# Two diagonal cells joined into one, and other places for the second keys, the inverses and the Gelu, in a two-layer transformer kernel

## What is computed

```
x = x + 0.5 * fp4_ffn(norm(x))          # weights and activations rounded to a 4-bit grid, width 352
x = x + linear_attention(norm(x))       # 16 heads of 64, and a feed-forward of width 512
x = x + 0.5 * fp4_ffn(norm(x))
x = x + 0.5 * relu_ffn(norm(x))         # width 512
x = x + causal_attention(norm(x))       # below
x = x + 0.5 * relu_ffn(norm(x))
```

```
scores = Q K^T + mask (causal);  attn = softmax(scores);  o = attn V
out = y + gelu(o) Wf + bf
```

## Time and profile before

| | us |
|---|---|
| timed runs | 1039.2, 1044.87, 1044.88 |
| median | 1044.87 |
| the profiled execution | 1038.98 |
| its span on the core | 1037.1 |

### The profile page before, as it was taken

One profiled execution on the slowest core, in us unless ns is written; L12 is line 12 of the kernel. 1 busy time (PEld: TensorE's weight loads), 2 busy tenths in 40 slices (PEclk: granted clock), 3 DMA queues, 4 the chain that ended last, 5 costly groups with the idle time before them and its releaser, 6 DMA issues.

```text
span 1037.1 us, 19863 instructions
## 1 busy us (share of the span) xinstructions
PE 902.4 (87%) x7281; PEld 449.5 (43%) x7281; DVE 695.6 (67%) x1678; ACT 510.4 (49%) x889; POOL 260.5 (25%) x409
## 2 busy tenths in 40 slices
PE   3689997887888787867898989999999999999997
PEld 1455545666676575423443433243332233332225
DVE  7899824467887766549764677765679767677204
ACT  1333332234445332444556555756656666666774
POOL 3566410234555654203240001222000000000000
PEclk9999998989999987888999999999999999999999
DMA  8100000000000050040012100000500000000000
GB/s 211 44 1 1 1 1 1 1 1 0 2 1 1 2 92 1 8 87 13 13 53 39 38 15 17 12 3 14 91 22 11 10 4 5 16 5 12 5 9 12
DMA packets 30699, 22.66 MB, mean 22 GB/s; under 512 B 9530, under 2 KB 27786, under 8 KB 30604
## 3 DMA queue, kind: packets, MB, share of 16 engines
q1 hardware_dynamic: 28660, 20.84, 9.2%
q10 hardware_dynamic: 1944, 0.55, 0.3%
HBM read 16.79 MB, written 4.32 MB: 20 GB/s over the span
## 4 chain that ended last, share of the span: by engine, by line
PE 59%; DVE 22%; ACT 6%; issue 6%; POOL 5%; DMA 1%; SPq 0%; ACTq 0%; DVEq 0%; POOLq 0%
PE psum L1756 12%; PE psum L1773 11%; PE psum L1730 7%; PE psum L1695 5%; DVE arena L1347 5%; PE psum L1642 3%; ACT arena L1000 3%; PE psum L1611 2%; PE psum L1449 2%; PE psum L1653 2%; POOL rs L721 2%; PE psum L1787 2%; PE psum L1540 2%; PE psum L1676 1%; DVE arena L1220 1%
## 5 line engine op out<-in xcount | busy, mean ns | idle before, releaser
L1347 DVE TENSOR_REDUCE arena<-psum 128x2 f32<-128x1024 f32 (+2 forms) x320 | 336.1, 1064 | 142.8 <-PE psum L1695 79.2
L1000 ACT ACTIVATE arena<-psum 128x1024 f32<-128x1024 f32 (+3 forms) x320 | 284.5, 897 | 157.6 <-PE psum L1730 82.7
L721 POOL TENSOR_TENSOR rs<-ve,mhalf 128x1 f32<-128x1 f32 x128 | 71.9, 568 | 358.0 <-DVE ve L1129 357.6
L1756 PE MATMUL psum<-arena 128*32 128x512 f32 (+3 forms) x1280 | 153.5, 552 | 1.3 <-ACT arena L1000 1.3
L1773 PE MATMUL psum<-arena,ones 128*32 128x512 f32 (+3 forms) x1280 | 150.2, 541 | 0.9 <-DVE arena L1374 0.8
L1695 PE MATMUL psum<-arena 48*128 48x512 bf16 (+3 forms) x640 | 111.7, 352 | 26.8 <-DVE arena L1347 10.4
L1730 PE MATMUL psum<-arena 50*128 50x512 bf16 (+3 forms) x640 | 114.3, 357 | 16.0 <-DMA arena<-arena 9.1
L1730 PEld LDWEIGHTS psum<-arena 50*128 50x128 bf16 x640 | 31.1, 93 | 195.3 <-issue 115.3
L828 POOL TENSOR_TENSOR arena<-arena 128x512 f32<-128x512 f32 x15 | 19.1, 1272 | 232.1 <-DMA arena<-scr_sums 232.1
L969 ACT ACTIVATE rh<-psum,fb 128x128 f32<-128x128 f32 x128 | 36.5, 368 | 58.6 <-PE psum L1642 58.6
L1695 PEld LDWEIGHTS psum<-arena 48*128 48x128 bf16 x640 | 35.7, 94 | 54.1 <-DVE arena L1347 19.3
(11 more groups left out here) (193 smaller groups left out, 1470.7 us busy)
## 6 DMA issues: line engine op xcount, KB each, us to landing
arena<-scr_parts SPq DMA_DIRECT2D x96, 64.0 KB
arena<-scr_sums SPq DMA_DIRECT2D x60, 64.0 KB, 2.0
scr_parts<-arena SPq DMA_DIRECT2D x12, 256.0 KB, 2.6
arena<-arena SPq DMA_DIRECT2D x124, 2.0 KB, 1.7
X<-in_L_attn_src_dram SPq DMA_DIRECT2D x4, 256.0 KB, 4.6
out_dram<-X SPq DMA_DIRECT2D x16, 64.0 KB, 1.6
arena<-in_L_attn_Wk_dram SPq DMA_DIRECT2D x1, 512.0 KB, 6.8
arena<-in_L_attn_Wq_dram SPq DMA_DIRECT2D x1, 512.0 KB, 7.7
```

The source lines that it names most:

```text
L721: v.tensor_tensor(rs[:, u, t:t + 1], ve[:, u, t:t + 1], mhalf[:, :], ALU.pow).then_inc(s_rstd[u], 1)
L1000: v.activation(pr[:, u % RING, pp, :, 0:CH - off], both(("scores", n))[0][:, :, off:CH], ACT.Exp).then_inc(s_p, 1)
L1347: v.tensor_reduce(MXP[:, j, 2 * pp:2 * pp + 2, m], both(("max", g, pp, j, m))[0][:, :, 0:hi - lo], AX_X, ALU.max).then_inc(s_mxd, 1)
L1756: last = mm(bank(O_BANK)[VD * h:VD * h + VD, off:CH], V[kb // TPC][:, kb % TPC, GH * (g % GPC) + h, :], pr[:, u % RING, h // 2, h % 2, 0:C ...
```

## The change

In the groups 4 to 14 the diagonal is done in three cells instead of four, in the order 0, 2, (1, 3): key blocks 1 and 3, of 384 and 128 queries, share one cell as two **strips** of one PSUM bank and one exponential of 512 queries. The counts of cells and the places that are given in cells follow from it. The number tables change beside that. Line numbers of the new kernel are higher by 23 to 24 in most engines' parts.

```diff
-INVERT_AT, NORM_AT = {0: 5, 1: 3, 2: 3, 3: 3}, {0: 7, 1: 5, 2: 5, 3: 5}
-GELU_AT = {0: 11, 1: 8, 2: 8, 3: 1}
-RELU_BEHIND, RELU_TILE = 4, 4
+INVERT_AT = {0: 3, 1: 5, 2: 3, 3: 2}
+NORM_AT = {0: 5, 1: 6, 2: 5, 3: 7}
+GELU_AT = {0: 10, 1: 8, 2: 9, 3: 1}
+JOINED = [(0,), (2,), (1, 3)]
+JOINED_FROM = 4
+RELU_BEHIND = 4
+RELU_TILE = 3
...
-LOADS_PER_HALF = {1: 4, 2: 2, 3: 2}
+LOADS_PER_HALF = {1: 4, 2: 3, 3: 8}
...
-FIRST_SLOT = -12
-TAIL = {8: (-11, 1), 9: (-11, 1), 10: (-10, 1), 11: (-9, 1), 12: (2, 2), 13: (6, 2), 14: (12, 2), 15: (18, 2)}
-MAX_LEADS = {1: 2, 2: 3, 3: 3, 4: 3}
-SECOND_KEYS_START, SECOND_KEYS_EVERY = -9, 3
+FIRST_SLOT = -11
+TAIL = {8: (-11, 1), 9: (-11, 1), 10: (-10, 1), 11: (-9, 3), 12: (0, 2), 13: (5, 2), 14: (12, 2), 15: (18, 2)}
+MAX_LEADS = {1: 2, 2: 4, 3: 3, 4: 3}
+SECOND_KEYS_START = -11
+SECOND_KEYS_EVERY = 3
+LOADS_LATER = {1: 2, 2: 5, 3: 2}
...
-        CELLS = [(g, kb) for g in range(MGROUPS) for kb in range(TPC * (g // GPC + 1))]
-        GROUP_U = [CELLS.index((g, 0)) for g in range(MGROUPS)] + [len(CELLS)]
         LAST = MGROUPS - 1
+
+        def cells_of(g):
+
+            first = TPC * (g // GPC)
+            joined = JOINED if JOINED_FROM <= g < LAST else [(j,) for j in range(TPC)]
+            return [(kb,) for kb in range(first)] + [tuple(first + j for j in x) for x in joined]
+
+        CELLS = [(g, x) for g in range(MGROUPS) for x in cells_of(g)]
+        GROUP_U = [CELLS.index((g, cells_of(g)[0])) for g in range(MGROUPS)] + [len(CELLS)]
+
+        def strips(u):
+
+            g, x = CELLS[u]
+            at, out = CH, []
+            for kb in x:
+                off = P * max(kb - TPC * (g // GPC), 0)
+                at -= CH - off
+                out.append((kb, off, at))
+            return [(kb, off, a, a - at) for kb, off, a in out], at
...
-                    h = first + 1 + k // LOADS_PER_HALF[c]
+                    h = first + 1 + LOADS_LATER[c] + k // LOADS_PER_HALF[c]
...
             def exponentials(n):
                 u, pp = n // GP, n % GP
-                g, kb = CELLS[u]
-                off = P * max(kb - TPC * (g // GPC), 0)
+                off = strips(u)[1]
...
             def scores(n):
...
+                for kb, off, at, _ in strips(u)[0]:
+                    for par in range(2):
+                        r = slice(64 * par, 64 * par + MAX_ROW + 2)
+                        last = mm(o[:, par, at:at + CH - off], KK[kb // TPC][r, hp, P * (kb % TPC):P * (kb % TPC) + P],
+                                  QS[c % 2][r, hp, off:CH],
+                                  start=True, stop=(kb < TPC * c), skip_group_check=True)
...
             def values(u):
...
+                for kb, off, _, at in strips(u)[0]:
+                    for h in range(GH):
+                        last = mm(bank(O_BANK)[VD * h:VD * h + VD, off:CH],
+                                  V[kb // TPC][:, kb % TPC, GH * (g % GPC) + h, :],
+                                  pr[:, u % RING, h // 2, h % 2, at:at + CH - off], start=(kb == 0), stop=end,
+                                  skip_group_check=True)
```

More of the change, by code:

```diff
@@ L513, in causal @@
                         out.append(("values" if i == 0 else "sums", u - 1))
[L514 to L517, removed]
+                        g, x = CELLS[u - 1]
+                        if g == LAST and x[0] >= TPC * (CHUNKS - 1):
+                            out.append(("take_tile" if i == 0 else "invert_tile", x[0] % TPC))
+                        elif u == GROUP_U[g + 1]:
                             out.append(("take_o" if i == 0 else "take_d", g))
@@ L1719, in scores @@
                 u, pp = n // GP, n % GP
-                g, kb = CELLS[u]
+                g, x = CELLS[u]
                 c, hp = g // GPC, GP * (g % GPC) + pp
-                off = P * max(kb - TPC * c, 0)
-                if (kb, pp) == (0, 0):
+                if (x[0], pp) == (0, 0):
                     pe.wait_ge(s_mq[g % 2], 16 * GH * (g // 2 + 1))
@@ L1743, in values @@
             def values(u):
-                g, kb = CELLS[u]
+                g, x = CELLS[u]
                 c = g // GPC
-                off = P * max(kb - TPC * c, 0)
-                end = kb == TPC * (c + 1) - 1
-                if (g % GPC, kb) == (0, 0):
+                end = u + 1 == GROUP_U[g + 1]
+                if (g % GPC, x[0]) == (0, 0):
                     pe.wait_ge(s_vc, TPC * (c + 1))
-                if kb == 0:
+                if x[0] == 0:
                     B[O_BANK].free(pe)
-                if g == LAST and kb > TPC * (CHUNKS - 1):
-                    pe.wait_ge(s_otl, kb - TPC * (CHUNKS - 1))
+                if g == LAST and x[0] > TPC * (CHUNKS - 1):
+                    pe.wait_ge(s_otl, x[0] - TPC * (CHUNKS - 1))
                 pe.wait_ge(s_p, GP * (u + 1))
-                for h in range(GH):
-                    last = mm(bank(O_BANK)[VD * h:VD * h + VD, off:CH], V[kb // TPC][:, kb % TPC, GH * (g % GPC) + h, :],
-                              pr[:, u % RING, h // 2, h % 2, 0:CH - off], start=(kb == 0), stop=end,
-                              skip_group_check=True)
+                for kb, off, _, at in strips(u)[0]:
[4 more added lines that the diff above has]
+                                  skip_group_check=True)
                 last.then_inc(s_av, 1)
@@ L1763, in sums @@
             def sums(u):
-                g, kb = CELLS[u]
+                g, x = CELLS[u]
                 c = g // GPC
-                off = P * max(kb - TPC * c, 0)
-                end = kb == TPC * (c + 1) - 1
-                if kb == 0:
+                end = u + 1 == GROUP_U[g + 1]
+                if x[0] == 0:
                     B[D_BANK].free(pe)
-                if g == LAST and kb > TPC * (CHUNKS - 1):
-                    pe.wait_ge(s_dtl, kb - TPC * (CHUNKS - 1))
-                for h in range(GH):
-                    last = mm(bank(D_BANK)[VD * h:VD * h + VD, off:CH], ones1[:, 0:VD],
-                              pr[:, u % RING, h // 2, h % 2, 0:CH - off], start=(kb == 0), stop=end,
-                              skip_group_check=True)
+                if g == LAST and x[0] > TPC * (CHUNKS - 1):
+                    pe.wait_ge(s_dtl, x[0] - TPC * (CHUNKS - 1))
+                for kb, off, _, at in strips(u)[0]:
+                    for h in range(GH):
+                        last = mm(bank(D_BANK)[VD * h:VD * h + VD, off:CH], ones1[:, 0:VD],
+                                  pr[:, u % RING, h // 2, h % 2, at:at + CH - off], start=(kb == 0), stop=end,
+                                  skip_group_check=True)
                 last.then_inc(s_dn, 1)
```

17 lines of the change are left out of this document (6 added, 11 removed).

## The result

The changed kernel takes 1015.46 us (median of 4 runs, 1013.92 to 1017.91), the kernel before beside it 1043.03 (4 runs, 1039.2 to 1044.88): ratio 0.9753, 95% interval 0.972 to 0.9787. The profiled execution took 1015.57 us (span 1013.8) against 1038.98 (span 1037.1), 23.4 less.

A forecast was written before the change was run, and what follows sets the result against it. TensorE, busy 87% of the span, was taken as the bound, with an 8.8 us DMA wait before group 2's scores. Terms summed to 13.5 us: 1025.5 from the profiled run, 1031.4 from the median; forecast 1028, range 1017 to 1041.

The forecast's parts named there:

- Part 1: Second chunk's keys and group 2's maxima issued sooner: the 8.8 us wait shrinks to some 2, gaining 7.5 us.
- part 5: Third and fourth chunks' loads, Gelu and feed-forward tiles at other places: -0.4 us, ends -4 and 1.
- Part 2: TensorE's clock after the stall, 1.2 GHz from 460 to 470 us: 0.7 us gained, ends 0 and 3.9.
- part 4: The opening, one slot fewer ahead of the first scores, tile 11 finished slower: 1.0 us gained, ends -4 and 7.
- Part 3: Joined cells in groups 4 to 14: 4.0 us from fewer changes between matmul kinds, 0.7 from VectorE's maxima.
- A: Rival: the wait changes hands to VectorE and strips pay their change; 1034 us, from the median 1040; chance 0.24.
- B: Rival: new waits put 450 to 510 us in a low-clock, short-chain state; slower, 1045.5 us; chance 0.08.
- C: Rival: more gain from full strips, no key wait, a shorter opening and half the clock; 1019 us; chance 0.10.

The follow-up runs named there:

- keys alone: The kernel before with only first slot, tail, maxima of group 2 and the second chunk's keys at their new places; 1024.61 us, ratio 0.9818.
- keys and joins: The kernel before with the new second keys, maxima and opening and the joined cells, all other places as before; 1023.72 us, ratio 0.985.
- the kernel without joined cells: The changed kernel with four diagonal cells again in every group and feed-forward tiles every four cells; 1029.19 us, ratio 0.9854.
- the opening alone: The kernel before with only first slot and tail at their new places, tile 11 finished later; 1033.75 us, ratio 0.994.
- the two last kernels: The kernel before, values and sums of full cells in groups 8 to 15 split, one-column matmul between strips in their shape or the scores'; 1049.73 and 1083.56 us.
- the keys of before: The changed kernel with first slot, tail, maxima of group 2 and second chunk's keys and loads at their old places; 1030.61 us, ratio 0.9875.

## Why the forecast was too small

| term | forecast | measured in profiled executions |
|---|---|---|
| 1, the stall | 7.5 | 7.26: idle time in the groups 0 to 3 (19.60 to 12.34) |
| 2 and 4, clock and opening | 1.7 | 4.66: 3.89 ahead of group 0, 0.77 less busy in the groups 0 to 3 |
| 3, joined cells | 4.7 | 4.99: groups 4 to 14, keys alone against keys and joins |
| 5, other places | −0.4 | 5.89: groups 4 to 14, keys and joins against the whole change, 1.7 of it clock |
| none | 0 | 0.71: groups 4 to 14, before against keys alone |
| sum | 13.5 | 23.51 |

**Part 1 was right in mechanism and size.** The 8.77 us are gone, 2.67 stay at the first wide maximum of group 4, as forecast ("some 2 us"), and the loads stand right behind the maxima of group 1. The loads start 8.5 us sooner than I wrote (430.91 for 439.4) and the keys come 5.1 sooner (454.60 for 459.7), since the maxima of group 1 are turned sooner and the opening is shorter; group 4's own place moved with them, so the wait is that of the forecast. The reciprocal of group 0 waited 0.94 us for its gather, where I allowed up to 3. That of group 9, some 4 in the forecast of part 5, waited 3.29, and TensorE lost nothing. For the second the kernel without joined cells shows that it was luck of the place: there the gather landed hardly later after its issue (14.5 us against 13.3), but VectorE stood 10.05 us for it and TensorE stopped.

**Part 2 was mis-sized, and part 4 with it.** I priced the clock only between 463 and 472 and took 0.7. The clock's loss before was larger and lay elsewhere too: 0.70, 0.79 and 0.73 between 400 and 430. With the new keys and opening alone TensorE is at 1.2 GHz for 22.4 us less, and 6.6 us of busy time go; the forecast had 1.7 us for clock and opening together. The argument that VectorE's 9.69 of 10 would hold the stretch behind the stall fell: with VectorE at 9.59 of 10 from 460 to 470 the kernel with the keys alone still keeps all of the 16 us that it has at group 2, to 15.3 at the end. That idleness lets the clock fall and work brings it back, the rule that I set beside the term (the Trainium skill, TensorE: Matmul & The Clock Gate, The HAM clock gate), would have given 3.2 us more and was nearer to the runs than my choice, though the lower level didn't vanish but stood at other places (0.66 from 470 to 480 in the whole change). How the 6.6 us split into the opening's chains and the keys isn't sharp. From 375 to group 0, kernels with the same opening spent from 8.9 to 13.7 us at 1.2 GHz; the whole change had 11.9. One pair can't tell the opening's worth either: the seven kernels with the new first slot and tail reach group 0 at 415.0 to 422.8 us, on the mean 418.7, the five with the old ones and the old keys at 422.4 to 426.9, on the mean 424.5. That is some 6 us, and the opening alone has 6.2 by its timed ratio, where part 4 had 1.0.

**Part 3 came out right by two errors that cancel.** The stretch of the groups 4 to 14 gets 5.0 us shorter by the joins in both pairs (6.7 less 1.7 of clock against before, 4.99 with the keys), where I had 4.7. But it is made of 6.9 to 7.1 us less busy time, where I took 4.0 and called 5.5 the most, and of 2.0 to 2.1 us more idle time, where I took 0.7 less for VectorE's maxima. Between the starts of the groups 4 and 15 TensorE changes tile shape 540 times in the changed kernel instead of 584, two for each of the 22 half slots, and one change costs 0.21 / 2 = 0.105 us, so 44 of them are 4.6 us; the other 2.3 to 2.5 stay open. My reason for taking less than the full price, that two strips might pay between each other, is refuted with 0.01 us. That a change of tiling mode drains the engine and a change of tile doesn't (the Trainium skill, TensorEngine Tiling (Array Packing), Key Properties) fits the weight loads of the two last kernels, and the 5.5 by that rule was the better value.

**Part 5 was wrong in sign.** I looked for waits that the moved steps could cause and found none, and gave no worth to places that fit the new length of the groups. Joining takes two half slots from each group, and idle time rises (20.0 us with the keys alone, 22.2 with keys and joins); with inverse, Gelu, tiles and loads placed anew it is 18.3. That the lost half slots were cover for it is my reading and not shown. Put in one at a time, inverse and Gelu take 1.7 us off and the tiles 0.2; the other 1.9 need the loads or all at once. Without the joined cells the same places with eight loads per half slot collide with group 9's gather and make the stretch 475.41 us, 8.8 longer than before; with two loads per half slot the timed runs (0.9845) can't be told from those of the keys alone (0.9818), so it is the loads that do the harm there, as far as this pair shows. The terms 3 and 5 aren't separate: together they give 11.6 us in the whole change, and 12.1 with the keys of before (466.66 to 454.60).

**The level.** The profiled execution of before stood some 4 us below its median, that of after at its own. I had named a middle between the two levels; the timed difference of 27.6 us is 23.4 and this 4.

**The rivals.** A (the wait changes hands) has against it that the gain at group 2 stays to the end in the kernel with the keys alone, 16.0 and 15.3 us. B (the clock falls for 60 us) didn't come, but its mechanism is there on a small scale where a gather waited 10 us: 0.58 over 10 us. C, with 1019 us, was nearest, and had its terms from the right places: full price of the strips, more clock, a shorter opening.

## What to carry to other kernels

Where a wait of several microseconds goes, read the granted clock of the 60 us around it in the rows of before and price every stretch at 1.2 GHz that could be work at 2.4, not only the one behind the wait. Count changes of tile shape on TensorE, not instructions: joining two small pieces of the same shape into one turn saved 0.2 us each time here. When a change shortens a repeated stretch, the places of the side work have to be fitted anew, and that fitting has a worth of its own that belongs to the sum; here it was 4.2 us without the clock, beside 5.0 for the joins.

## What the runs showed of the hardware

A change of TensorE's tile shape between 128 rows by 32 and 64 rows by 128 cost 0.105 us each way, one more strip and small matmul within a shape 0.01 us. Within a shape the next weights were loaded 0.21 us ahead of their matmul, across a change only as it began (891.11 for 891.32, 901.43 for 901.43). The granted clock in a stretch of short chains isn't fixed: the profiled executions of kernels with the same opening differ by up to 4.7 us in their time at 1.2 GHz, and 10 executions of one kernel (the opening alone) took 1030.36 to 1037.29 us at mean clocks of 0.964 to 0.973. And four small transfers of a gather, issued behind 24 key loads on one queue, let the reciprocal that needs them start 14.5 us after their issue (729.04 to 743.50), in the whole change 13.3 us after it (719.02 to 732.33).
